# A Mamba block between two ternary feed-forwards: the low fp16 halves of transposed tiles are subtracted by VectorE instead of by a matmul and a ScalarE copy

## The reference

```
x = x + 0.5 * (layernorm(x) @ w_tern.T + bias)       # w_tern: 1024 x 1024, ternary times a scale
x = x + mamba(layernorm(x))
x = x + 0.5 * (layernorm(x) @ w_tern.T + bias)       # the same weights

mamba: u, z = split(x @ W_in.T);  u = silu(conv4(u));  dt_r, B, C = split(u @ W_xproj.T)
       dt = softplus(dt_r @ W_dt.T + b_dt)
       h[t] = exp(dt[t] * A) * h[t-1] + dt[t] * B[t] * u[t]     # 1024 channels x 16 states
       y = (sum over states of C[t] * h[t] + u * Dskip) * silu(z)
       return y @ W_out.T
```

## Time and profile before

| | |
|---|---|
| time, median of 3 runs | 3150.39 us (3149.94 to 3152.36) |
| time of the profiled execution | 3149.94 us |
| its span in the trace | 3148.2 us |
| busy: VectorE | 2680.9 us (85%), 3463 instructions |
| busy: TensorE | 2488.0 us (79%), 12448 matmuls |
| busy: ScalarE | 1812.2 us (58%) |
| busy: GpSimd | 1775.2 us (56%) |
| granted TensorE clock, mean | 0.90 of full |

### The profile page before, as it was taken

The page is one execution under the profiler, slowest core; times in us unless marked ns, Lnnn a source line. Parts: engine busy times, 40 slices in busy tenths (PEclk is TensorE's granted clock), DMA queues, the critical chain, the costliest instruction groups (busy, mean ns, idle before and its releaser), DMA issues.

```text
span 3148.2 us, 42154 instructions
## 1 busy us (share of the span) xinstructions
PE 2488.0 (79%) x12448; PEld 1418.5 (45%) x12448; DVE 2680.9 (85%) x3463; ACT 1812.2 (58%) x3286; POOL 1775.2 (56%) x1497
## 2 busy tenths in 40 slices
PE   2578889888888546888878878887888887888887
PEld 1233444444433234555545445554454554555553
DVE  6566766776776579999999999999999999999993
ACT  2234766676676745566556565555665655655653
POOL 1111322222221167687787787877877877877873
PEclk8789999999998667899999999899999999898999
DMA  6543323323322261122121221221221212212101
GB/s 211 198 181 121 139 77 115 135 74 122 128 76 100 95 248 68 38 85 70 59 76 57 81 75 55 88 72 58 71 85 45 75 59 85 71 61 81 44 27 41
DMA packets 152840, 286.79 MB, mean 91 GB/s; under 512 B 40128, under 2 KB 89536, under 8 KB 148224
## 3 DMA queue, kind: packets, MB, share of 16 engines
q1 hardware_dynamic: 152576, 283.71, 26.6%
HBM read 174.09 MB, written 109.58 MB: 90 GB/s over the span
## 4 chain that ended last, share of the span: by engine, by line
POOL 27%; issue 20%; DVE 14%; PE 1%; POOLq 1%; ACT 1%; DMA 0%; DVEq 0%; SPq 0%; ACTq 0%
POOL dbu L1019 20%; DVE h L1197 9%; DVE y L1207 4%; POOL x L1043 2%; POOL o L1049 2%; POOL y L1039 1%; POOL dbu L1024 1%; POOL carry L1030 1%; PE p_g L1320 1%; POOLq L40 1%; PE p_g L1310 0%; POOL small L69 0%; DVE q L1220 0%; DVE x L1231 0%; DMA edge_dt<-dt_scratch 0%
## 5 line engine op out<-in xcount | busy, mean ns | idle before, releaser
L1106 ACT ACTIVATE p_da<-dt,neg_a 128x255 f32<-128x255 f32 x2048 | 887.9, 468 | 724.1 <-DVE h L1197 723.9
L1197 DVE TENSOR_TENSOR_SCAN h<-p_da,dbu 128x512 f32<-128x512 f32 x1024 | 1191.7, 1205 | 26.2 <-POOL dbu L1024 15.3
L1019 POOL TENSOR_TENSOR dbu<-dtu,bb 128x1024 f32<-128x1024 f32 x512 | 1197.8, 2361 | 0.8 <-issue 0.2
L1286 PE MATMUL p_ht<-ident,h 128*128 128x128 f32 x4096 | 618.9, 310 | 220.3 <-DVE h L1197 217.9
L1286 PEld LDWEIGHTS p_ht<-ident,h 128*128 128x128 f32 x4096 | 542.6, 161 | 333.8 <-issue 174.8
L1207 DVE SCALAR_TENSOR_TENSOR y<-p_ht,ct,y 128x1024 f32<-128x1024 f32 x512 | 645.3, 1260 | 1.5 <-PE p_ht L1286 1.5
L706 PE MATMUL p_u<-xz,wu 128*128 128x512 f16 x1536 | 351.8, 387 | 0.0
L1329 PE MATMUL p_g<-wz,xz 128*128 128x512 f16 x1536 | 348.9, 384 | 0.0
L1320 PE MATMUL p_g<-wo,tokt 128*128 128x512 f16 x1536 | 347.4, 383 | 1.6 <-ACT tokt L1127 1.6
L358 POOL TENSOR_TENSOR late<-dt,u 128x512 f32<-128x512 f32 x64 | 82.3, 1286 | 424.7 <-DVE dt L550 424.7
L69 POOL TENSOR_TENSOR small<-small,consts 128x1 f32<-128x1 f32 x96 | 56.9, 592 | 438.3 <-DVE small L62 426.8
(11 more groups left out here) (115 smaller groups left out, 2814.6 us busy)
## 6 DMA issues: line engine op xcount, KB each, us to landing
bb<-b_scratch SPq DMA_DIRECT2D x128, 256.0 KB, 3.3
xin<-in_x SPq DMA_DIRECT2D x32, 512.0 KB, 4.3
x_scratch<-x SPq DMA_DIRECT2D x32, 512.0 KB, 3.3
xz_scratch<-xz SPq DMA_DIRECT2D x16, 1024.0 KB, 5.8
y_scratch<-late SPq DMA_DIRECT2D x32, 512.0 KB, 2.9
dt_scratch<-dt SPq DMA_DIRECT2D x64, 256.0 KB, 2.2
dtu_scratch<-late SPq DMA_DIRECT2D x64, 256.0 KB, 2.5
dt<-dt_scratch SPq DMA_DIRECT2D x16, 1024.0 KB, 7.3
```

The source lines that it names most:

```text
L1019: nc.gpsimd.tensor_tensor(state[:, 4 * f:4 * f + 4, :], dtu[par][:, 4 * f:4 * f + 4, :], bb[n // NB % 2][:, n % NB:n % NB + 1, :].to_broad ...
L1106: ins_ = nc.scalar.activation(p_da[p % 2][:, k * T2 + 1:(k + 1) * T2], dt[par][:, g, 1:], ACT.Exp, scale=neg_a[:, g, n:n + 1])
L1197: nc.vector.tensor_tensor_scan(h[n % 2][:, 2 * p:2 * p + 2, :].rearrange("p g t -> p (g t)"), p_da[p % 2][:], dbu[n % 2][:, 2 * p:2 * p + ...
L1286: mm = nc.tensor.transpose(p_ht[t][:, g * P:(g + 1) * P], h[n % 2][:, g, t * P:(t + 1) * P], ident[:])
```

## The change

Steps 3 and 4 of the split are replaced by one instruction. `take_high`, ScalarE's `low`, `minus_ident`, the semaphores `minus_set` and `hi_taken` and the table `halves_before` go. VectorE gets a `low` that waits for `hi_done`, subtracts part 0 from the bank, writes part 1 and raises `g_free`. It stands at the end of slots 4, 7, 10 and 15, behind the second addition of a state; in the tail, where there are no scans, it stands in the same order among what is left. Since nothing is added to a bank after the transposes any more, these are written as `transpose` and no longer as matmuls with start and stop flags.

```diff
--- before.py
+++ after.py
@@ -802,7 +802,6 @@
         x1 = [sb(f"x1_2{t}", [P, D]) for t in range(TT2)]
         q = [sb(f"q{i}", [P, HALF]) for i in range(2 * TT2)]
         tokt = sb("tokt", [P, 2, G, P], F16)
-        minus_ident = sb("minus_ident", [P, P], F16)
         xn = sb("xn_2", [P, D])
         o = [sb(f"o{i}", [P, HALF]) for i in range(2)]
         small = sb("small2", [P, 48])
@@ -833,7 +832,6 @@
         g_free = [sem(f"g_free{i}") for i in range(2)]
         th_done, gate_done = sem("th_done"), sem("gate_done")
         tok_chain, tok_scale, y_scaled, hi_done = (sem(n) for n in ("tok_chain", "tok_scale", "y_scaled", "hi2_done"))
-        minus_set, hi_taken = sem("minus_ident_set"), sem("hi2_taken")
         ln_chain, stats_ready, pow_done, scale_ready, xn_done = (
             sem(n) for n in ("ln2_chain", "stats2_ready", "pow2_done", "scale2_ready", "xn2_done"))
         xb_done, fin_done = sem("xb2_done"), sem("fin_done")
@@ -846,14 +844,6 @@
                8: [("o", 1, 0)], 9: [("o", 1, 1)], 10: [("n", 0, 0), ("n", 0, 1)], 13: [("f", 0, 0)],
                14: [("f", 0, 1)], 15: [("n", 1, 0), ("n", 1, 1)]}
         ZED = {2: [("z", 0, 0)], 3: [("z", 0, 1)], 11: [("z", 1, 0)], 12: [("z", 1, 1)]}
-
-        HALVES = {("t", 0): 0, ("t", 1): 2, ("n", 0): 4, ("n", 1): 6}
-
-        def halves_before(i, n):
-
-            return [(j, kind, t) for on, j, kind, t in
-                    ((flags(i)[1] and n == 5, i, "t", 0), (flags(i)[1] and n == 8, i, "t", 1),
-                     (flags(i)[1] and n == 11, i, "n", 0), (flags(i)[0] and n == 0, i - 1, "n", 1)) if on]
 
         def flags(i):
 
@@ -1120,13 +1110,6 @@
                         nc.scalar.activation(tokt[:, 0, 4 * x:4 * x + 4, :], p_g[b][:].rearrange("p (g t) -> p g t", g=4),
                                              ACT.Copy).then_inc(hi_done, 1)
 
-                def low(i, kind, t):
-                    for x in range(2):
-                        b, m = place(i, kind, t, x)
-                        wait(act, hi_taken, (i - 1) * 8 + HALVES[kind, t] + x + 1)
-                        nc.scalar.activation(tokt[:, 1, 4 * x:4 * x + 4, :], p_g[b][:].rearrange("p (g t) -> p g t", g=4),
-                                             ACT.Copy).then_inc(g_free[b], 1)
-
                 def scale_y(c, cpar, t):
                     wait(act, tok_scale, c * TT2 + t + 1)
                     nc.scalar.activation(y[cpar][t][:], y[cpar][t][:], ACT.Copy, scale=gs[t][:, 3:4]).then_inc(y_scaled, 1)
@@ -1148,8 +1131,6 @@
                     e_on, c_on, z_on = flags(i)
                     c = i - 1
                     for n in range(NS):
-                        for unit in halves_before(i, n):
-                            low(*unit)
                         if z_on:
                             decays(i, par, n, (0, 1))
                         if e_on and n in (1, 2):
@@ -1186,7 +1167,6 @@
                         for k in range(2):
                             nc.vector.memset(p_da[b][:, k * T2:k * T2 + 1], 0.0).then_inc(da_zeroed, 1)
                     dve.wait_ge(da_zeroed, 4)
-                    nc.vector.tensor_scalar(minus_ident[:], ident[:], -1.0, None, ALU.mult).then_inc(minus_set, 1)
 
                 def scans(i, n, half):
                     if half == 0:
@@ -1219,6 +1199,15 @@
                     wait(dve, th_done, i * 4 + 2 * t + x + 1)
                     nc.vector.scalar_tensor_tensor(out=q[2 * t + x][:], in0=q[2 * t + x][:], scalar=1.0, in1=p_g[b][:],
                                                    op0=ALU.add, op1=ALU.mult).then_inc(g_free[b], 1)
+
+                def low(i, kind, t):
+
+                    before = {("t", 0): 0, ("t", 1): 2, ("n", 0): 4, ("n", 1): 6}[kind, t]
+                    for x in range(2):
+                        b, m = place(i, kind, t, x)
+                        wait(dve, hi_done, (i - 1) * 8 + before + x + 1)
+                        nc.vector.tensor_tensor(tokt[:, 1, 4 * x:4 * x + 4, :], p_g[b][:].rearrange("p (g t) -> p g t", g=4),
+                                                tokt[:, 0, 4 * x:4 * x + 4, :], ALU.subtract).then_inc(g_free[b], 1)
 
                 def add_product(i, t, x):
 
@@ -1266,6 +1255,8 @@
                         if c_on:
                             if n in (2, 3):
                                 token_scale(i - 1, 1 - par, n - 2)
+                            if n in (4, 7):
+                                low(i, "t", n // 7)
                             if n in (8, 11):
                                 t = n // 11
                                 for x in range(2):
@@ -1273,6 +1264,8 @@
                                     wait(dve, g_free[b], m + 1)
                                 row_stats(dve, nc, x1[t], stats, mv, vn, small[:, 40:41], ln_chain, stats_ready,
                                           scale_ready, (i - 1) * TT2 + t)
+                            if n in (10, 15):
+                                low(i, "n", n // 15)
 
                 drive(dve, body, prologue)
 
@@ -1300,8 +1293,7 @@
                             wait(pe, xn_done, (i - 1) * TT2 + t + 1)
                         for k in range(4):
                             g = 4 * x + k
-                            mm = nc.tensor.matmul(p_g[b][:, k * P:(k + 1) * P], src[:, g * P:(g + 1) * P], ident[:],
-                                                  start=(k == 0), stop=(k == 3), is_transpose=True)
+                            mm = nc.tensor.transpose(p_g[b][:, k * P:(k + 1) * P], src[:, g * P:(g + 1) * P], ident[:])
                     if kind == "f":
                         for a in range(2):
                             wait_evac(i - t, "n", t, a)
@@ -1331,15 +1323,6 @@
                                 n += 1
                     mm.then_inc(g_full[b], 1)
 
-                def take_high(i, kind, t):
-                    if isinstance(i, int) and i == 1:
-                        pe.wait_ge(minus_set, 1)
-                    for x in range(2):
-                        b, m = place(i, kind, t, x)
-                        wait(pe, hi_done, (i - 1) * 8 + HALVES[kind, t] + x + 1)
-                        nc.tensor.matmul(p_g[b][:], minus_ident[:], tokt[:, 0, 4 * x:4 * x + 4, :],
-                                         start=False, stop=True, skip_group_check=True).then_inc(hi_taken, 1)
-
                 def wait_evac(i, kind, t, a):
                     b, m = place(i, kind, t, a)
                     wait(pe, g_free[b], m + 1)
@@ -1348,8 +1331,6 @@
                     e_on, c_on, z_on = flags(i)
                     seq = sequence(i)
                     for n in range(NS):
-                        for half in halves_before(i, n):
-                            take_high(*half)
                         if n and z_on:
                             turn_state(i, n - 1)
                         if n == 0 and c_on:
```

## The result

The changed kernel takes 3207.75 us (median of 4 runs, 3205.63 to 3210.02) against 3150.16 us before (also of 4 runs, one more than in the table of the kernel before); the ratio is 1.0182, 95% interval 1.0165 to 1.0200. Forecast were 3213 us, with a range of 3206 to 3226. The profiled execution took 3209.26 us, its span is 3207.4 us, 59.2 more than before. Lines have moved: the scan is line 1177 (1197 before), the addition of a state 1187 (1207), the decays 1096 (1106), GpSimd's product 1009 (1019), ScalarE's fp16 copy 1110 (1120), and VectorE's new subtraction is line 1209.

What follows compares the result with a forecast made beforehand. The prediction took VectorE to bound the kernel while scans run. Subtractions 70.8, less 6.5 of waits and 1.4 in the tail, made +62.9 us on 3149.94: 3212.8, given as 3213, range 3206 to 3226.

Steps and rivals of the forecast that it cites:

- What bounds the kernel: Second pass, 1200 to 3060 us: VectorE bounds, busy 1842.7 of 1860 us; time added to it during scans shows in full.
- The sign named for it: ScalarE and GpSimd each wait some 60 us longer for scans, ScalarE more still by its 67 us of lost copies.
- The subtractions: Second pass, while scans run: 118 subtractions added to VectorE at 0.60 us each, 70.8 us.
- No wait at the new places: Ends of slots 4, 7, 10, 15: ScalarE's fp16 copies are ready 2.0 us early, so VectorE's wait costs nothing.
- When the bank and the tile come free: Behind slot 7's pair: VectorE frees them later, TensorE's next product starts about 0.3 us later, costing nothing.
- What comes back: VectorE's nine waits for decays, put down to low copies and TensorE's matmul ahead of them, vanish: 6.5 us back.
- The upper bound of 10.3: Most that could come back, in us: all of VectorE's idle time before scans; the lower bound was 0.
- The tail: After the last scan: one subtraction replaces matmul and copy, saving 0.35 us at each of four hand-overs, 1.4 us.
- Rival 1: Subtractions fall into VectorE's gaps, only the gains stay: 3142 us; chance 2 in 100.
- Rival 2: VectorE waits at the subtractions for ScalarE, 0.5 us for each of 59 pairs: 3242 us; chance 4 in 100.
- Rival 3: GpSimd's product and the subtraction block one another, 85 us more: 3298 us; chance 3 in 100.
- Rival 4: The time stays as it is, the extra work covered, needing 63 us of cover; chance 1 in 100.

Runs made afterwards that it cites:

- e2: The changed kernel with a second subtraction, over 384 of 512 columns into an unread scratch tile, ahead of each one: 3274.82 us, ratio 1.0392 to the kernel before.
- e6: The changed kernel with all four pairs of subtractions ahead of their slots' second scans instead of at the slot's end: 3263.32 us, ratio 1.0364 to the kernel before.
- e4: The kernel before without TensorE's matmul; ScalarE copies the value a second time, so low halves are not the remainder: 3148.82 us, ratio 0.9992.
- e7: e3 with the loop of six rounds of two turns made three rounds of four: 3142.46 us, ratio 0.9976 to the kernel before.
- e8: e3 with eight more VectorE waits on a long-raised semaphore in slot 7 of every turn: 3144.36 us, one run.
- e9: e3 with 24 more VectorE waits on a long-raised semaphore in slot 7 of every turn: 3142.10 us, one run.
- e3: The kernel before with ScalarE's low copies moved behind the slot's first two decays, TensorE's matmul kept: 3143.56 us, ratio 0.9976.
- e1: The changed kernel without its subtractions: part 1 zeroed once, ScalarE's fp16 copy frees the bank: 3143.01 us, ratio 0.9974 to the kernel before.
- e5: The changed kernel with slot 15's pair of subtractions moved behind the first scans of the next turn's slot 0: 3209.15 us, ratio 1.0192 to the kernel before.

## Why the forecast was right

**What bounds the kernel.** Right. Every run that put work or waits on VectorE paid for it almost in full (e2, e6), and the runs that took work from ScalarE and TensorE alone gained little or nothing (e4). The sign named for it came: GpSimd waits 63 us longer for scans (some 60 forecast), ScalarE 146 (127 forecast). The margin to the next engine is small, though: e7, e8 and e9 have lost e3's gaps at the returns and yet end with it, between 1947.4 and 1948.5 us of scans, mostly because TensorE's transposes are then late. The forecast said that VectorE "waits for nearly nobody", and didn't ask who would be next.

**The subtractions.** Forecast 118 x 0.60 = 70.8 us. From start to start they hold VectorE 0.598 us (1.195 us a pair), 70.5 us in all, and e1 prices them at 64.75 us. The term was right as a price on an engine that is always busy; 5.8 us of it were paid with gaps that the kernel without them has. The record of 0.682 us would have given 80.5; the spacing decides for 0.60. The figure of 691 ns of the Trainium skill ("VectorE: DVE Perf Modes", section on the TRN2 errata) describes the record, within 2% here too, and not what the engine is held for.

**No wait at the new places.** Right: no wait of VectorE for a copy ahead of the last scan, with 1.5 to 2.6 us in hand where the forecast read 2.0; e6 shows that without them it would have been 42 us.

**When the bank and the tile come free.** Right in its effect alone. The product behind slot 7's pair starts 2.5 us after the place of the pair (2314.48 to 2316.98), where it was 1.06 before; that is 1.4 us later and not 0.3, since the 16 transposes ahead of it took 3.62 us at a granted clock of 0.53, and 2.19 at 1.00 before. Nobody waits for it.

**What comes back.** This is the mis-sized term: 6.5 us forecast, 9.2 measured (70.5 - 61.35), and the reason given for most of it was wrong. The size first: the view names only waits over 0.15 us, and each gap also ends an overlap of 0.08 us. From start to start the five returns cost the kernel before 5.0 us and 18 waits in the middle of turns 3.9; all are gone in the changed kernel, which makes nearly the whole of the 9.2. The upper bound of 10.3 held it. Then the reason. The forecast put all nine waits down to TensorE's late matmul and the low copies ahead of the decays. That holds for the waits in the middle of a turn; e3 shows that the copies' place alone is worth 4.4 us. It doesn't hold for the five gaps at the loop's returns (the earlier trace rows shows one of them), the larger part of the 6.5 us. They stay when the copies move (e3), when the matmul goes (e4) and when both go (e1), and vanish with idle instructions on VectorE (e8, e9) or another loop (e7). In the changed kernel they are not missing because the hand-over is, since e1 has no hand-over and has the gaps. What is left between the two is VectorE's code, the subtractions, and not their place ahead of the jump (e5); that it is the same cause as in e8 and e9 is concluded and not shown. That this part of the 6.5 us came back was therefore luck. Their absence is a gain there and hardly one in e7 to e9: with 9 us more work for VectorE in each round of the loop TensorE is no longer late anywhere (no wait of VectorE for it in the stretch), so the shorter gaps count in full.

**The tail.** The step was right, 0.35 to 0.36 us for three of the hand-overs against 0.35 forecast (0.46 for the first), and the term of 1.4 us didn't show in the span, since one product ran 1.7 us longer at TensorE's lower clock and two others 0.3 together. Such a product occurs in the kernels without the change too (e3), and the size of the forecast's term is below the scatter of the tail.

**The rivals.** Rival 1 (gaps take the subtractions) is refused by e1: they take 5.8 of 70.5 us. Rival 2 (waits at the subtractions) by the trace; e6 gives its price. Rival 3 (GpSimd and the subtraction block one another) by durations: 678 to 692 ns over all 128 subtractions, 118 of which lie within a running product of GpSimd by the trace, and 2.36 us for that product in both kernels. That is how the port rule of "SBUF — State Buffer" in the Trainium skill would have it for an operation with one input in PSUM.

Rival 4 (the time stays) falls with the 57.6 us.

The sum: forecast +62.9, measured +57.6 in the medians and +59.2 in the spans. Of the 3.7 us between +62.9 and +59.2, the terms explain it so: subtractions -0.3, what comes back -2.7, tail +1.8, the part before the first scan -2.6, which is scatter; together -3.8.

**A better version.** e3 and e7 beat both kernels, by 0.24% over the kernel before (intervals from 0.14 to 0.34%) and, by the ratios, 2.0% over the changed one. e3 is the smaller edit: one loop of two lines moved behind another.

## What to carry to other kernels

Price an instruction that moves to the engine that bounds by the start-to-start time of the same form elsewhere in the trace, and multiply; on an engine that was busy 99% of the time it came out at nine tenths of that here (e1), with gaps of the engine making up the rest. Ask at what distance the next engine follows: once 4 or 5 us of 1950 were taken from VectorE's gaps here, TensorE was mostly the one that was late, and three further edits gave 1 us at most. When a wait is named after an engine, check that engine's end against the waiter's start; what of a gap lies behind the releaser's end is not that engine's work.

## What was not expected of the hardware

- VectorE's gap at the return of a loop depends on its own code: 0.7 to 1.1 us at each return in e3, 0 with 16 or 48 more idle instructions in the loop, 0 with a loop of four turns instead of two (e7), 1.7 to 1.9 us with a second subtraction and its wait at each of eight places a turn (e2), 0 in the changed kernel. A shorter wait of VectorE for itself, once a round, moves in the same way: 0.15 us at the token scale in the kernel before, 0.31 at the row statistics in the changed one, 0.31 at another place of the token scale in e8, none in e9.
- Up to 24 waits a turn on a semaphore long raised cost VectorE nothing that can be seen: by the starts of its reductions a round of the loop takes 244.6 to 245.8 us with them (e9) and 245.5 to 246.0 without (e3), and in e9 slot 8's first scan, right behind the 24 waits, starts 1.17 or 1.18 us after the addition, as elsewhere.
- TensorE's granted clock fell to 0.57 for 4 us within the last product of the changed kernel, after a pause of 1.51 us, and stayed at 1.00 in e4 after 1.75 us and in e2 after 2.17 us of pause in the same place; in e3 it fell to 0.57 for 4 us in the product before the last, after a pause of 0.78 us.
